# Behind the first attention of a graph network: LayerNorm work moved from VectorE to ScalarE, and edge comparisons cut to near keys

## The reference

```
edge_index = stack([src, dst])
x = layernorm(x + L0(x, edge_index))   # graph attention, 8 heads, then selu
x = layernorm(x + L1(x, edge_index))   # three layers: relu(relu((x + sum of x[src]) @ wa + ba) @ wb + bb)
x = layernorm(x + L2(x, edge_index))   # graph attention, 4 heads, skip, layernorm with gain and offset
x = layernorm(x + L3(x, edge_index, edge_weight))   # three weighted graph convolutions

layernorm(x) = (x - mean) / sqrt(var + 1e-5)
selu(v) = 1.0507 * (max(v, 0) + 1.6733 * (exp(min(v, 0)) - 1))
```

## Time and profile before

| | us |
|---|---|
| median of 3 runs | 7126.04 (7118.27 to 7150.4) |
| profiled execution | 7125.99 |
| its span, first to last instruction | 7124.2 |

### The profile page before, as it was taken

The page is one execution under the profiler, slowest core; times in us unless marked ns, Lnnn a source line. Parts: engine busy times, 40 slices in busy tenths (PEclk is TensorE's granted clock), DMA queues, the critical chain, the costliest instruction groups (busy, mean ns, idle before and its releaser), DMA issues. The chain is left out here.

```text
span 7124.2 us, 38615 instructions
## 1 busy us (share of the span) xinstructions
PE 3212.4 (45%) x11661; PEld 2005.2 (28%) x11661; DVE 3269.2 (46%) x5638; ACT 1783.3 (25%) x1855; POOL 3459.4 (49%) x3338
## 2 busy tenths in 40 slices
PE   3000000000000079999999500000015999999999
PEld 2000000000000057777778400000013444544544
DVE  5565555698687723445657344444446000000111
ACT  1233333100000056666667322222210000000000
POOL 3677777677667755556667277777730000000000
PEclk8555555555555589999999755555557999999999
DMA  3355555209950056433358333333323888888887
GB/s 108 137 206 172 188 175 185 93 0 329 372 219 0 0 174 210 151 106 111 111 163 251 122 99 110 98 106 102 102 70 104 284 293 294 288 293 294 294 299 261
DMA packets 502441, 1242.14 MB, mean 174 GB/s; under 512 B 114227, under 2 KB 162841, under 8 KB 493273
## 3 DMA queue, kind: packets, MB, share of 16 engines
q1 hardware_dynamic: 382408, 1114.01, 45.8%
q0 software_dynamic: 119824, 125.65, 7.4%
HBM read 861.79 MB, written 377.50 MB: 174 GB/s over the span
## 5 line engine op out<-in xcount | busy, mean ns | idle before, releaser
L361 POOL DMA_INDIRECT gb<-rows,src x1564 | 1589.8, 1017 | 679.0 <-issue 548.5
L754 PE MATMUL psum<-gb,big 128*128 128x512 f32 (+1 forms) x3822 | 1579.3, 568 | 3.0 <-DVE gb L778 2.0
L593 POOL DMA_INDIRECT plane<-total,cell x782 | 836.4, 1070 | 558.0 <-DVE gb L574 192.9
L1108 ACT CAST strips<-gb 128x1024 fp32r<-128x1024 f16 (+1 forms) x764 | 805.1, 1077 | 1068.2 <-DMA gb<-plane 913.9
L1820 PE MATMUL psum<-identity,end_top 128*8 128x128 f32 (+1 forms) x2 | 0.8, 375 | 2277.6 <-issue 1173.9
L593 POOL DMA_INDIRECT plane<-begun,cell x782 | 831.9, 1064 | 338.9 <-issue 236.1
L1091 PE MATMUL psum<-strips,high 128*128 128x512 f32 (+1 forms) x1274 | 398.9, 401 | 1269.1 <-DVE strips L778 1252.9
L754 PEld LDWEIGHTS psum<-gb,big 128*128 128x128 f32 x3822 | 691.5, 190 | 770.9 <-issue 770.9
L556 DVE SCALAR_TENSOR_TENSOR psum<-gb,psum 128x782 f32<-128x782 f32 x782 | 756.8, 1032 | 211.4 <-remote 136.6
L1820 PEld LDWEIGHTS psum<-identity,end_top 128*8 128x8 f32 (+1 forms) x2 | 0.2, 82 | 2278.3 <-issue 1174.3
L1805 ACT COPY gb<-turned 128x1632 f32<-128x1632 f32 (+3 forms) x138 | 450.7, 3266 | 727.6 <-DVE turned L1893 514.6
(11 more groups left out here) (305 smaller groups left out, 3754.9 us busy)
## 6 DMA issues: line engine op xcount, KB each, us to landing
gb<-plane SPq DMA_DIRECT2D x588, 512.0 KB, 4.5
gb<-plane SPq DMA_DIRECT2D x294, 576.0 KB, 4.8
plane<-turned SPq DMA_DIRECT2D x49, 3200.0 KB
gb<-plane SPq DMA_DIRECT2D x588, 256.0 KB
gb<-plane SPq DMA_DIRECT2D x294, 288.0 KB
plane<-turned SPq DMA_DIRECT2D x49, 1600.0 KB
runs<-gb SPq DMA_DIRECT2D x33, 1748.0 KB
runs<-gb SPq DMA_DIRECT2D x33, 1610.0 KB
```

The costliest lines, as they stand in the source:

```text
L361: m.s_rows[b % BUFS].up(nc.gpsimd.indirect_dma_start(m.batch(b, columns, row)[:, j, 0:width], None, table, bass.IndirectOffsetOnAxis(ap=m. ...
L593: done.up(m.nc.gpsimd.indirect_dma_start(plane, bass.IndirectOffsetOnAxis(ap=m.cell[:, r:r + 1], axis=0), total[:, r:r + 1], None), 16)
L754: mm = nc.tensor.matmul(m.psum[:, self.bank(r, 0, i), 0:nodes], rows, slot[:, a:a + nodes], start=(s == 0), stop=False)
L1108: m.s_strip_act.up(nc.scalar.copy(out, landed))
```

## The change

In `count_edges` a comparison reads the keys of columns 0 to `near` alone, where `near` is 69 columns past the group's start ((b + 3) x 23, at most 782), instead of all 782.

In `selu_stage` ScalarE takes over the positive part with its scale (one operation of 6272 elements), the squares with their sum (49 operations of 128 elements, one for each tile, each with an accumulator), and the centering together with the scaling (49 more). VectorE folds the constants into two operations with a scalar and two tensors, and keeps the sum of the mean and small operations of 49 elements. Groups 7 and 8 are counted while ScalarE squares and scales; before, group 7 was counted while it made the high part.

```
 def count_edges(m, dve, first, last):
     for b in range(first, last):
+        near = min(COLS, (b + BUFS) * NARROW)
         for r in range(b * NARROW, (b + 1) * NARROW):
             m.s_compared.up(nc.vector.scalar_tensor_tensor(
-                m.unread[r % 2], m.key, m.key[:, r:r + 1], m.step[:, COLS - 1 - r:2 * COLS - 1 - r], ALU.is_equal, ALU.mult,
+                m.unread[r % 2][:, 0:near], m.key[:, 0:near], m.key[:, r:r + 1], m.step[:, COLS - 1 - r:COLS - 1 - r + near], ALU.is_equal, ALU.mult,
                 accum_out=m.total[:, r:r + 1]))
@@ selu_stage, vector
             m.s_dve_turn.up(nc.vector.tensor_scalar(scratch, out, 0.0, None, ALU.min))
             dve.wait_ge(m.s_act_turn.sem, m.s_act_turn.at(1))
-            c.link(nc.vector.tensor_scalar(scratch, scratch, -1.0, SELU_SCALE * SELU_ALPHA, ALU.add, ALU.mult))
-            c.link(nc.vector.tensor_tensor(x, x, scratch, ALU.add))
-            c.link(nc.vector.tensor_scalar(out, out, 0.0, SELU_SCALE, ALU.max, ALU.mult))
-            c.link(nc.vector.tensor_tensor(x, x, out, ALU.add))
-            center(m, c, x, scratch)
-            rescale(m, c, dve, x, 2)
+            c.link(nc.vector.scalar_tensor_tensor(x, scratch, SELU_SCALE * SELU_ALPHA, x, ALU.mult, ALU.add))
+            dve.wait_ge(m.s_act_turn.sem, m.s_act_turn.at(2))
+            c.link(nc.vector.scalar_tensor_tensor(x, out, -SELU_SCALE * SELU_ALPHA, x, ALU.add, ALU.add))
+            c.link(nc.vector.tensor_reduce(m.mean[:, :], x, AX.X, ALU.add))
+            m.s_dve_turn.up(nc.vector.tensor_scalar(m.mean[:, :], m.mean[:, :], -1.0 / D, None, ALU.mult))
+            count_edges(m, dve, COUNTED_AHEAD, COUNTED_AHEAD + 1)
+            dve.wait_ge(m.s_act_turn.sem, m.s_act_turn.at(3))
+            m.s_dve_turn.up(nc.vector.tensor_scalar(m.var[:, :], m.var[:, :], 1.0 / D, LN_EPS, ALU.mult, ALU.add))
+            dve.wait_ge(m.s_act_turn.sem, m.s_act_turn.at(4))
+            c.link(nc.vector.reciprocal(m.var[:, :], m.var[:, :]))
+            m.s_dve_turn.up(nc.vector.tensor_tensor(m.mean[:, :], m.mean[:, :], m.var[:, :], ALU.mult))
+            count_edges(m, dve, COUNTED_AHEAD + 1, COUNTED_AHEAD + 2)
+            dve.wait_ge(m.s_out.sem, m.s_out.at(1))
...
-            count_edges(m, dve, COUNTED_AHEAD, COUNTED_AHEAD + 1)
             dve.wait_ge(m.s_parts.sem, m.s_parts.at(1))
             m.s_split.up(nc.vector.tensor_tensor(m.low_part[:, :, :], x, rounded, ALU.subtract))
-            count_edges(m, dve, COUNTED_AHEAD + 1, COLS // NARROW)
+            count_edges(m, dve, COUNTED_AHEAD + 2, COLS // NARROW)
@@ selu_stage, scalar
             m.s_act_turn.up(nc.scalar.activation(scratch, scratch, ACT.Exp))
-            root(m, act, 2)
+            m.s_act_turn.up(nc.scalar.activation(out, out, ACT.Relu, scale=SELU_SCALE))
+            act.wait_ge(m.s_dve_turn.sem, m.s_dve_turn.at(2))
+            for t in range(TILES):
+                square = nc.scalar.activation(scratch[:, t, :], x[:, t, :], ACT.Square, bias=m.mean[:, t:t + 1],
+                                              accum_out=m.var[:, t:t + 1])
+            m.s_act_turn.up(square)
             root(m, act, 3)
+            act.wait_ge(m.s_dve_turn.sem, m.s_dve_turn.at(4))
+            for t in range(TILES):
+                normed = nc.scalar.activation(x[:, t, :], x[:, t, :], ACT.Identity, bias=m.mean[:, t:t + 1], scale=m.var[:, t:t + 1])
+            m.s_out.up(normed)
+            root(m, act, 5)
             act.wait_ge(m.s_out.sem, m.s_out.at(1))
```

More of the change, by code:

```diff
@@ L2013, in _ @@
+            dve.wait_ge(m.s_act_turn.sem, m.s_act_turn.at(4))
[3 more added lines that the diff above has]
+            dve.wait_ge(m.s_out.sem, m.s_out.at(1))
             m.s_dve_turn.up(nc.vector.tensor_scalar(m.var[:, :], m.dinv[:, :], 1e-30, None, ALU.max))
             c.link(nc.vector.tensor_scalar(m.mean[:, :], m.dinv[:, :], 0.0, None, ALU.is_gt))
-            dve.wait_ge(m.s_act_turn.sem, m.s_act_turn.at(3))
+            dve.wait_ge(m.s_act_turn.sem, m.s_act_turn.at(5))
```

## The result

The changed kernel took 7099.89 us, median of 13 runs (7085.36 to 7112.01), against 7118.27 for the kernel before (13 runs, 7086.16 to 7163.68): ratio 0.9965, interval 0.9951 to 0.9980. That is 25 us faster by the ratio, inside the half per cent that the prediction called no change, where 121.5 us were forecast. The profiled execution took 7101.91 us, its span 7100.1, which is 24.1 us shorter than before.

The account below looks back on a forecast made before the run. GpSimd's scatters were taken to bound the stage before plane 0's first strip, lengthened by VectorE, with TensorE bounding what follows. Removing 98.6 us of waits and 22.9 us of held scatters gave 7126.0 - 121.5 = 7004.5 us, range 6986 to 7045.

Parts of the forecast that it names:

- Waits of GpSimd for counts: Scatters of plane 0: shorter comparisons keep VectorE ahead, so GpSimd's 12 waits for its counts go, saving 98.6 us.
- Rival 1: Counting from group 9: late starts are a limit per instruction, 1.42 us a comparison whatever its length; 7013 us, chance 0.10.
- Rival 2: Groups 2 to 8: a late stretch where VectorE has little lead makes GpSimd wait up to 40 us; 7045, chance 0.10.
- The held scatters: Scatters prolonged beside VectorE's operations: moving LayerNorm work to ScalarE gives back 22.9 us, leaving about 808 us busy.
- Rival 3: VectorE's new three-operand operations leave scatters free, a further gain of 12.4 us; 6992 us, chance 0.12.
- Rival 4: Late starts become the rule in counting, 2.8 us apart, and GpSimd waits in every group; 7806 us, chance 0.03.
- The start of the stage: VectorE still leaves the attention's block at 1425.30 us, when GpSimd reaches its branch; cost and gain 0.
- The node chain: LayerNorm work on VectorE and ScalarE: `x` ready near 1562 us instead of 1620, hidden beside scatters, so no cost.
- What follows the first strip: After plane 0's first strip loads: TensorE-bound, moves earlier as a whole and takes the same 4589 us.

Follow-up runs that it names:

- e6: Changed kernel with the wipe of plane 1 put off until all groups are counted; 6803.95 us in one run, on a chip of the second, faster kind.
- e1: Changed kernel with every comparison reading all 782 keys again, so the LayerNorm part alone; 7115.66 us, ratio 0.9954 to the kernel before.
- e2: Kernel before with only the shorter comparisons (near keys) added, LayerNorm work as before; 7115.67 us, ratio 0.9958.
- e3: Changed kernel with each comparison reading at most 115 keys; 7101.79 us, ratio 0.9940 to the kernel before.
- e7: Changed kernel with one more instruction (a wait for two values long reached) on GpSimd before each scatter, second kind of chip; 6779.27 us, ratio 0.9944.
- g2: Changed kernel with GpSimd's scatters from group 2 on put off until VectorE has counted all groups, first kind of chip; 7513.43 us in one run.
- h1: Changed kernel with scatters from group 2 on put off until all is counted, GpSimd kept busy with 1200 small fills meanwhile; 7538.86 us.
- g3: Changed kernel with one more instruction on GpSimd before each scatter, first kind of chip; 7116.64 us, ratio 0.9995 to the kernel before.
- e4: Changed kernel with at most 115 keys a comparison, waiting for an earlier one only once in eight columns; 7097.76 us, ratio 0.9929.
- g4: Changed kernel counting several groups at once by shifted keys, with far fewer instructions, first kind of chip; 7119.48 us, ratio 1.0007.

## Why the prediction was wrong, point by point

The forecast of 7004.5 us and the chance of 0.95 for a time under 7090.4 were wrong. The range began at 6986 and ended at 7045, and 7099.89 lies 55 us above it.

- *The step that failed* is "Waits of GpSimd for counts", worth 98.6 of the 121.5 us: waits for L567 of 0 to 4 us were forecast, and 110.1 were measured. It took the 251 us of late stretches as a fixed time to which the shorter comparisons add: 427 + 251 = 678 us for groups 9 to 33. They took 825.5. On the chips without late starts the first number holds: 427 us of comparisons and small operations were forecast, and 427 measured (e6: 427.2), ahead of which lie 21.5 us for the low part and its waits, 448.7 together. What failed was the assumption on the second number. It isn't fixed: in e1, e2 and e3 shorter comparisons got more idle time, and the pace stayed at 1.4 to 1.5 us each. Without late starts (e6, e7) the waits were 0.0 us, as forecast, so the step would have held on a chip of the second kind; there, however, the kernel before had only 8.6 us of them to give back.
- *Rival 1* named this mechanism and gave it 0.10, but its price was too low, for it let VectorE start group 9 at 1575 with a lead of four groups. VectorE got there at 1682, when GpSimd was in group 8. At 33.0 us a group against GpSimd's 29.3 a lead that isn't there never comes, and GpSimd waits about every third group. What the prediction had against it, the 180 comparisons that ran without a late start, shows that it is no fixed price of an instruction; e3 shows that the average is one all the same. "The stretches come irregularly" was said against it too; in e3 they come every five groups.
- *Rival 2* came true beside it: late starts in groups 4, 5 and 8, with waits of 13.0 us at group 5 and 10.6 at group 8. That "before, groups 2 to 8 had none" was taken as a property of the place.
- *The held scatters* were right: 22.9 us forecast, 26.3 measured, 805.6 busy against "about 808". *Rival 3* fell: scatters of 6.29 and 6.42 us beside the two three-operand operations. Here the Trainium skill ("SBUF — State Buffer", section "Who interferes with whom") says that descriptor generation needs the write interface, inferred from a tensor_tensor that stalled nothing. This trace differs from that inference, as it did before the change, and now for three-operand operations too.
- *Rival 4*, slower, didn't happen: the pace stayed below its limit of 1.62 us a comparison.
- *The start of the stage* was right (1425.38). *The node chain* was 108 us late, where g2, without late starts, had it 8 us early, and hidden, as forecast, behind 420 us of slack. *What follows the first strip* was right: 4580.7 and 4587.1 us against 4589.

The Trainium skill ("Runtime: NRT & Kernel Launch", section "Instruction fetch mechanics") says that fetching is mostly hidden because an engine takes instructions more slowly than they come. The runs agree in g2, h1 and on the second kind of chip. On the first kind beside scatters VectorE stood idle up to 4.16 us ahead of a comparison of 0.34 us (e3), but that this idle time is fetching was not shown, and the packets of instructions above speak against slow ones.

*Open:* what joins indirect DMAs to the starts on other engines, and why two of the five chips don't show it. That ScalarE is struck at the same time, and that g3 was slower, would fit something that the engines' queues share; the equal packets of instructions speak against the bringing of the instructions itself. The waits aren't it: e4, with an eighth of them, was only 6 us quicker than e3. Of the versions tried e4 had the lowest ratio on the first kind (0.9929, 0.9906 to 0.9952); its interval overlaps that of the changed kernel.

## What to carry to other kernels

When an engine shows idle time that its releasers don't explain, don't put it into a sum as a fixed amount: shortening its instructions may only lengthen the gaps. Before shortening them, run once with the suspected neighbour's work put off, which here took one wait and showed beside which work the gaps stand. And take the same kernel's profile on a second chip before explaining a stall: here the whole term on which the forecast stood, 98.6 us, was 8.6 us on another.

## What the runs showed of the hardware

- The same kernel took 7120 to 7181 us on three chips and 6814 and 6818 on two, some 4% less, with equal instructions: scatters of a mean of 1064 and 1063 ns, comparisons of 1032 ns. Of the 312.6 us between the two profiled spans (7124.2 and 6811.6) the first scatter has 77.2 (1363.40 and 1286.17), the stage 92.8, and what follows the rest. Over the whole kernel the 1564 gathers of the two attentions, also indirect DMAs of GpSimd, were shorter by 96.0 us and stood idle 70.5 us less (first kind, then second):

```profile
L361 POOL DMA_INDIRECT gb<-rows,src x1564 | 1589.8, 1017 | 679.0 <-issue 548.5 <-DMA rows<-big 97.6 <-DMA runs<-gb 32.9
```

```profile
L361 POOL DMA_INDIRECT gb<-rows,src x1564 | 1493.8, 955 | 608.5 <-issue 475.2 <-DMA rows<-big 97.7 <-DMA runs<-gb 35.7
```

- Late starts: mostly 2.1, 2.8 or 3.5 us from one comparison to the next, whatever its length from 0.34 to 1.04 us, on VectorE and (1.4 us apart) on ScalarE; in the counting they stood only beside indirect DMAs of GpSimd, and only on the one kind of chip.
- VectorE left the block only when GpSimd's queue got to its branch, some 12 scatters ahead of the scatter then running: 13.87 us of waiting before, 35.5 after, to the same instant (1425.3). Work put ahead of it can be free, or, as in g4, hold GpSimd for 45.9 us.
- The wipe of plane 1 took 390.5 us without scatters beside it (g2) and 430.0 with them.
